# A six-stage transformer: the light sum, the dense attention's schedule and the first expert gathers reordered

## The reference, cut to what matters

```python
x = x + half * routed_ffn(norm(x))      # f1: light local attention (windows of 128, 8 heads of 64) + heavy attention on routed tokens
x = x + latent_attention(norm(x))       # la: causal, 16 heads of 8, rotary
x = x + half * routed_ffn(norm(x))      # f2: as f1
x = x + half * experts(norm(x))         # m1: 64 experts of up to 48 tokens, plus a shared ffn
x = x + cosine_attention(norm(x))       # ca: 16 heads of 8, q and k normalised, dense softmax over 512 keys, output bias bo
x = x + half * experts(norm(x))         # m2: as m1
```

## Time and profile before

| | |
|---|---|
| median of 3 runs | 3302.72 us (3302.44 to 3307.93) |
| the profiled execution's own time, its span | 3303.23 us, 3301.5 us |
| PE, DVE, ACT, POOL busy | 85%, 70%, 56%, 45% of the span |
| exponentials of f1l, of f2l (first to last start) | 65.4 to 525.0, 1601.6 to 2089.7 us |
| exponentials of la | 901.8 to 1534.4 us |
| scatters of m1, of m2 | 2487.3 to 2584.2, 3196.6 to 3293.2 us |
| exponentials of ca | 2675.7 to 3052.2 us |

### The profile page before, as it was taken

One profiled execution on the slowest core, in us unless ns is written; L12 is line 12 of the kernel. 1 busy time (PEld: TensorE's weight loads), 2 busy tenths in 40 slices (PEclk: granted clock), 3 DMA queues, 4 the chain that ended last, 5 costly groups with the idle time before them and its releaser, 6 DMA issues. The chain is left out here.

```text
span 3301.5 us, 72698 instructions
## 1 busy us (share of the span) xinstructions
PE 2797.7 (85%) x24552; PEld 1869.8 (57%) x24552; DVE 2312.4 (70%) x6126; ACT 1849.4 (56%) x3771; POOL 1476.8 (45%) x1662
## 2 busy tenths in 40 slices
PE   7999998997699999998888999799785278887774
PEld 4777886775233333333567777677663145555642
DVE  5887776884588888883677777599662267786641
ACT  3777664553166666664577666455541257776421
POOL 1222236883455555542122223578555354451445
PEclk9999998998599999998999999899895579999775
DMA  2000000001333333320000000000162255553532
GB/s 80 1 0 1 0 0 1 0 0 31 77 78 79 79 79 81 87 68 14 14 0 0 1 0 0 1 0 0 50 164 35 82 138 124 135 127 88 142 86 31
DMA packets 158029, 162.92 MB, mean 49 GB/s; under 512 B 43264, under 2 KB 136064, under 8 KB 157056
## 3 DMA queue, kind: packets, MB, share of 16 engines
q1 hardware_dynamic: 148032, 148.24, 17.5%
q0 software_dynamic: 9216, 7.87, 1.8%
q10 hardware_dynamic: 576, 4.19, 0.3%
HBM read 84.57 MB, written 74.60 MB: 48 GB/s over the span
## 5 line engine op out<-in xcount | busy, mean ns | idle before, releaser
L1721 DVE CUSTOM_DVE_ANT_0 la_ps<-la_ps,la_tri 128x512 f32<-128x512 f32 (+3 forms) x1024 | 480.4, 514 | 91.9 <-PE la_ps L1302 84.2
L1575 ACT ACTIVATE la_prob<-la_ps 128x512 f32<-128x512 f32 x640 | 374.0, 601 | 236.0 <-PE la_ps L1313 229.1
L371 POOL TENSOR_TENSOR f2l_prob<-f2l_prob,f2l_rec 128x512 f32<-128x512 f32 x128 | 132.2, 1054 | 364.2 <-DVE f2l_rec L550 364.2
L1202 POOL TENSOR_SCALAR_AFFINE_SELECT la_prob<-la_prob 128x512 f32<-128x512 f32 x256 | 159.4, 635 | 298.9 <-ACT la_prob L1575 298.7
L1302 PE MATMUL la_ps<-la_ks,la_qs 48*128 48x512 bf16 (+3 forms) x1024 | 255.3, 318 | 42.2 <-DVE la_mx L1721 26.9
L371 POOL TENSOR_TENSOR f1l_prob<-f1l_prob,f1l_rec 128x512 f32<-128x512 f32 x128 | 133.9, 1067 | 334.2 <-DVE f1l_rec L550 334.2
L1313 PE MATMUL la_ps<-la_qs,la_ks 50*128 50x512 bf16 (+3 forms) x1024 | 243.0, 311 | 4.4 <-ACT la_prob L1575 1.8
L1313 PEld LDWEIGHTS la_ps<-la_qs,la_ks 50*128 50x128 bf16 x1024 | 67.2, 94 | 234.3 <-ACT la_prob L1575 170.8
L1345 PE MATMUL la_ps_o<-la_prob,la_v 128*32 128x512 f32 (+3 forms) x2048 | 196.0, 456 | 0.0
L1719 DVE TENSOR_REDUCE ca_mx<-ca_ps 128x4 f32<-128x512 f32 x256 | 163.7, 680 | 39.8 <-PE ca_ps L1302 39.5
L1575 ACT ACTIVATE ca_prob<-ca_ps 128x512 f32<-128x512 f32 x256 | 140.4, 598 | 38.1 <-PE ca_ps L1313 36.2
(11 more groups left out here) (551 smaller groups left out, 7979.2 us busy)
## 6 DMA issues: line engine op xcount, KB each, us to landing
stack_image<-la_parts SPq DMA_DIRECT2D x192, 128.0 KB, 2.4
stack_image<-ca_parts SPq DMA_DIRECT2D x192, 128.0 KB, 2.3
la_qs<-stack_image SPq DMA_DIRECT2D x64, 192.0 KB, 3.5
la_ks<-stack_image SPq DMA_DIRECT2D x64, 192.0 KB, 4.4
ca_qs<-stack_image SPq DMA_DIRECT2D x64, 192.0 KB, 3.8
ca_ks<-stack_image SPq DMA_DIRECT2D x64, 192.0 KB, 4.8
gather_table<-m_xn SPq DMA_DIRECT2D x32, 256.0 KB, 2.3
gather_table<-m_pr SPq DMA_DIRECT2D x32, 128.0 KB, 2.3
```

What stands on the lines that cost most here:

```text
L371: nc.gpsimd.tensor_tensor(pr[:, g], pr[:, g], rc[:, g].rearrange("p (h o) -> p h o", o=1).broadcast_to([P, PAIRS, P]), ALU.mult).then_inc( ...
L1202: return nc.gpsimd.affine_select(view, view, pattern=[[0, 4], [1, P]], compare_op=ALU.is_ge, fill=0.0, base=0, channel_multiplier=-1)
L1575: nc.scalar.activation(prob[q % 2][:, n], ps2[n % 2][:], ACT.Exp, scale=SM).then_inc(S["p_sb"], 1)
L1721: last = nc.vector.tensor_tensor_reduce(bank[:, col:col + width], bank[:, col:col + width], tri[:, T - width:T], 1.0, -BIG, ALU.add, ALU.m ...
```

## The change

1. `light_attention`, DVE: the output sum y (L554) moves from behind the reciprocals to in front of the wait for the exponentials.
2. `stacked_attention`, dense form: the slots after every second unit become `place` after every unit, on PE, ACT and DVE, with the work spread over the 16 units; probabilities times v goes in two halves. The split of the maxima goes from DVE to POOL. The bias is added to y by POOL ahead of time (`add_bias`), and DVE's sum becomes one instruction; `added` goes. POOL's order in a body becomes one list. SP stores k's parts, loads the first half, sends the maxima rows, stores the next batch's q parts, then loads the second half. For the latent form only two empty instructions on POOL and some implied waits differ.
3. `moe_block`: SP writes the lists ahead of the store of base sum 12 and reads them back ahead of that of 13; POOL issues two gathers after each of base sums 13, 14 and 15.

The hunks of the dense attention are shown with the lines that stay and those that come; the lines that go are the `slot` functions and waits of the kernel as printed above.

```diff
@@ -541,6 +541,12 @@
                     if past(d, 1):
                         settle(d - 1)
                     descend(d)
+                if live(i, 3):
+                    dve.wait_ge(f_ps, i - 2)
+                    j = i - 3
+                    nc.vector.scalar_tensor_tensor(
+                        y[:, bass.ds(j, 1), :].rearrange("p o c -> p (o c)"), ps_a[:, 2], 0.5,
+                        x[:, bass.ds(j, 1), :].rearrange("p o c -> p (o c)"), ALU.mult, ALU.add).then_inc(y_ready, 1)
                 if live(i, 1):
                     dve.wait_ge(p_sb, i)
                     nc.vector.tensor_reduce(rsum[:], prob[(u - 1) % 2][:], X_AX, ALU.add).then_inc(sum_ready, 1)
@@ -548,12 +554,6 @@
                     if past(i, 3):
                         dve.wait_ge(norm_ready, 2 * i - 4)
                     nc.vector.reciprocal(rec[(u - 1) % 2][:], rsum[:]).then_inc(rec_ready, 1)
-                if live(i, 3):
-                    dve.wait_ge(f_ps, i - 2)
-                    j = i - 3
-                    nc.vector.scalar_tensor_tensor(
-                        y[:, bass.ds(j, 1), :].rearrange("p o c -> p (o c)"), ps_a[:, 2], 0.5,
-                        x[:, bass.ds(j, 1), :].rearrange("p o c -> p (o c)"), ALU.mult, ALU.add).then_inc(y_ready, 1)
                 if live(i, -2) and not late(i, r):
                     dve.wait_ge(xrT_ps, i + 2)
...
@@ -1141,26 +1140,39 @@
+                    if latent:
+                        store_parts(i + 2, u, 0)
+                    store_parts(i + 2, u, 1)
+                if latent and live(i, -1):
                     m_rows(i + 1, 1 - u, 0)
                 if live(i, -2):
                     sp.wait_ge(S["store_done"], 192 * (i + 3))
+                    load_half(i, u, 0)
+                if not latent and live(i, -1):
+                    m_rows(i + 1, 1 - u, 0)
+                if not latent and live(i, -3):
+                    store_parts(i + 3, 1 - u, 0)
+                if live(i, -2):
+                    load_half(i, u, 1)
+
+            def store_parts(b, u, t):
+                sp.wait_ge(S["part_ready"], 2 * b + 1 + t)
+                if t == 0 and past(b, 2):
                     for g in range(GROUPS):
+                        sp.wait_ge(load[g], 64 * (b - 1))
+                for blk, blks, part, stays in (RUNS_Q, RUNS_K)[t]:
+                    for k in range(blks):
+                        sp.dma_start(image[u, t, AD * (blk + k):AD * (blk + k + 1)].rearrange("d h t -> h d t"),
+                                     parts[:, t, part if stays else part + k]).then_inc(S["store_done"], 16)
+
+            def load_half(i, u, g):
+                if past(i, 0):
+                    sp.wait_ge(S["s2_ps"], UB * i + UB // 2 * (g + 1))
+                for t, stack in enumerate((qs[u], ks[u])):
+                    for s in range(2):
+                        r0, h0 = HALF_ROWS * s, PA * s + GP * g
+                        sp.dma_start(stack[r0:r0 + SROWS, GP * g:GP * g + GP, :], image[u, t, :, h0:h0 + GP, :])\
+                            .then_inc(load[g], 16)
 
             def m_rows(b, u, g):
                 sp.wait_ge(S["mT_sb"], 2 * b + 1 + g)
...
@@ -1228,16 +1242,27 @@
 
+            def add_bias(b):
+                pool.wait_ge(S["xn_ready"], b + 1)
+                nc.gpsimd.nop(nofuse=True)
+                ys = y[:, bass.ds(TPB * b, TPB), :]
+                nc.gpsimd.tensor_tensor(ys, ys, bo[:].broadcast_to([P, TPB, C]), ALU.add).then_inc(S["shifted"], 1)
+
             def body(i, u):
+                if not latent:
+                    if live(i):
+                        split_maxima(i, 1)
+                    if live(i, -2):
+                        split(i + 2, 1, 2, 5)
+                    if live(i, -1):
+                        split_maxima(i + 1, 0)
+                    if live(i):
+                        add_bias(i)
+                    if live(i, -3):
+                        split(i + 3, 0, 0, 5)
+                        split(i + 3, 1, 0, 2)
+                    return
                 for q in range(QUADS):
                     if live(i) and q == 0:
                         split_maxima(i, 1)
...
@@ -1473,62 +1508,49 @@
                 nc.tensor.matmul(ps_c[:], ones8[:], sq[:], start=True, stop=True).then_inc(S["sum_ps"], 1)
 
+            def place(i, u, q, n):
+                k = 4 * q + n
+                if k == 1:
                     if live(i):
                         m_t(i, 1)
                     if live(i, -3):
                         project(i + 3, 1 - u, 0)
+                if k == 4 and live(i, -3):
+                    project(i + 3, 1 - u, 1)
+                if k == 5 and live(i, -3):
+                    squares(i + 3, 0)
+                if k == 8:
                     if live(i, -3):
+                        squares(i + 3, 1)
                     if live(i, -1):
                         m_t(i + 1, 0)
+                if k == 9 and live(i, 1):
+                    turn_y(i - 1)
+                if k == 12 and live(i, 1):
+                    pe.wait_ge(S["yT_sb"], i)
                     if live(i, -3):
+                        pe.wait_ge(S["floored"], 2 * i + 8)
+                    else:
+                        pe.wait_ge(S["v_sb"], min(i + 2, B))
+                    for part in range(2):
+                        project_out(part)
+                if k == 13 and live(i, -4):
+                    xn_t(i + 4)
+                if n == 2:
+                    b, qb = (i, q - 2) if q >= 2 else (i - 1, q + 2)
+                    if live(i, 0 if q >= 2 else 1):
+                        otr(b, qb)
+                if n >= 2:
+                    b, qb, ub = (i, q - 1, u) if q else (i - 1, 3, 1 - u)
+                    if live(i, 0 if q else 1):
+                        pv(b, ub, qb, (0, 1) if n == 2 else (2, 3))
+                if k == 15 and live(i, -2):
+                    if live(i, -3):
+                        pe.wait_ge(S["floored"], 2 * i + 8)
                     if live(i, 1):
+                        pe.wait_ge(S["out_done"], i)
+                    for part in range(2):
+                        project_v(i + 2, u, part)
 
             def xn_t(b):
                 pe.wait_ge(S["xn_ready"], b + 1)
...
@@ -1608,21 +1629,28 @@
                 nc.scalar.copy(oT[:], ps_o[:]).then_inc(S["o_sb"], 1)
 
+            def place(i, u, q, n):
+                k = 4 * q + n
+                if k == 0 and live(i, -3):
+                    xnT_copy(i + 3, 1 - u)
+                if n == 0:
+                    b, qb = (i, q - 2) if q >= 2 else (i - 1, q + 2)
+                    if live(i, 0 if q >= 2 else 1):
+                        o_copy(b, qb)
+                if k == 2 and live(i, -3):
+                    biased(i + 3, 0)
+                if k in (3, 5) and live(i, -4):
+                    make_xn(i + 4, (k // 2 - 1,))
+                if k == 6 and live(i, -3):
+                    biased(i + 3, 1)
+                if k == 7 and live(i, -3):
+                    inverse(i + 3, 0)
+                if k == 9 and live(i, 1):
                     turned_y(i)
+                if k == 10 and live(i, -4):
+                    make_xn(i + 4, (2, 3))
+                if k == 11 and live(i, -3):
+                    inverse(i + 3, 1)
 
             def biased(b, t):
                 n = 2 * b + t
...
@@ -1707,7 +1735,7 @@
             def maxima(b, q, n):
-                if latent and n == 0 and q % 2 == 0 and past(b, 1):
+                if n == 0 and q % 2 == 0 and past(b, 1):
                     dve.wait_ge(S["m_ready"], 2 * b - 1 + q // 2)
                 dve.wait_ge(S["s1_ps"], UB * b + UQ * q + n + 1)
                 if latent:
...
@@ -1757,17 +1776,14 @@
                 out = ps_c[:].rearrange("p (a b) -> p a b", a=TPB)
+                if not latent:
+                    dve.wait_ge(S["shifted"], i)
+                    nc.vector.nop(nofuse=True)
+                nc.vector.tensor_tensor(ys, out, ys, ALU.add).then_inc(S["out_done"], 1)
 
...
@@ -1789,42 +1805,33 @@
 
+            def place(i, u, q, n):
+                k = 4 * q + n
+                if k == 1 and live(i):
+                    m_copy(i, 1)
+                if n == 3:
+                    b, qb = (i, q - 2) if q >= 2 else (i - 1, q + 2)
+                    if live(i, 0 if q >= 2 else 1):
+                        normalise(b, qb)
                 if k == 4 and live(i, -1):
+                    dve.wait_ge(S["v_ps"], i + 2)
+                    if live(i, 1):
+                        dve.wait_ge(S["pv_ps"], 4 * i)
+                    nc.vector.tensor_tensor(v[1 - u][:, :, :, 0:AD], ps_c[:].rearrange("p (j h d) -> p j h d", j=TPB, h=AH),
+                                            bv[:].rearrange("p o (h d) -> p o h d", h=AH).broadcast_to([P, TPB, AH, AD]),
+                                            ALU.add).then_inc(S["v_sb"], 1)
+                if k == 6 and live(i, -3):
+                    floor(i + 3, 0)
```

(32 more changed lines are left out.)

197 lines of the change are left out of this document (38 added, 159 removed).

## The result

The changed kernel took 3216.11 us in the median of 4 runs (3212.86 to 3218.55), the kernel before 3303.18 in the median of 4 beside them: the ratio is 0.9733, with a 95% interval from 0.9716 to 0.975. The profiled execution took 3215.8 us, 87.4 less than that of before. The forecast was 3224. The first row is the page's (busy us of each engine); the others are the exponentials of the two light blocks, first to last start.

What follows compares the result with a forecast made beforehand. It took DVE's ring, with PE in f2l's later passes, the first scatter's start, and PE's dense idle time as limits; 26 + 6 + 14 + 33 = 79 us off 3303.2, less 0.5, gave 3224 us, range 3188 to 3262.

Steps and rivals of the forecast that it cites:

- rivals A to D: A: dense body stays 24.5 us, 0.16; B: light gains only 9 us, 0.14; C: most idle returns, 0.08; D: slower, 0.07.
- 17 less 2.5: f2l descent: earlier make_xr and tmin gain 17 us; row sums standing behind y lose 2.5 us.
- Later passes: 0.30 x 39 = 12 us: f2l after the descent: PE's 0.30 us wait for y goes in 39 passes, gaining 12 us.
- Only if `make_xr` starts before POOL does ... I take the middle, 6: f1l descent: only an earlier make_xr start gains, 12 us; 6 taken, between a 2.5 loss and 12.
- this price of the gathers: Experts: sum 15, its store and gathers 5 and 6 come 2.6 us later, covered before the first scatter.
- The landing: Experts: the third gather, no longer beside the read-back, takes 3.5 us to land, so PE starts 7 us earlier.
- Half of PE's idle time: Dense attention: half of PE's lost 4.3 us a body recovered, 2.1 in each of 12 bodies, 25 us.
- start and tail: Dense attention: most of ACT's 7.87 us near the end with nothing from PE goes, 8 us.
- PE's waits for transfers: Dense attention: earlier loads remove PE's waits for the stacks from HBM, 15.3 us in 11 waits.
- DVE's 3.5 us: Dense attention: DVE loses maxima splits, one output sum and a port wait, about 3.5 of 19.4 us a body.
- Rival D: Dense attention: POOL's second maxima split runs late, delaying PE and SP's loads; body over 28.3 us, kernel slower; chance 0.07.
- Paced by DVE's 1024 maxima, and POOL is idle most of it: Latent attention: the waits removed, empty instructions and implied waits cost nothing there.

Runs made afterwards that it cites:

- one_product: The changed kernel with POOL's two light-attention products joined into one; 3239.17 us, ratio 0.9812 to the kernel before.
- sp_order_alone: The kernel before with only SP's new dense-attention order of stores and loads; 3292.97 us, ratio 0.9951 to the kernel before.
- splits_on_dve: The changed kernel with the dense splits of the maxima given back from POOL to DVE; 3215.52 us, ratio 0.9733 to the kernel before.
- loads_late: The changed kernel with the first half's dense loads issued behind the maxima's rows and the next q parts' store; 3365.07 us, ratio 1.0194 to the kernel before.
- sp_order_old: The changed kernel with all of SP's dense-attention order as before the change; 3226.29 us, ratio 0.9753 to the kernel before.
- xr_two_buffers: The changed kernel with a second xr buffer and make_xr moved ahead of the row sums; 3201.46 us, ratio 0.9694 to the kernel before.
- xr_before_y: The two-buffer xr kernel (make_xr ahead of the row sums) with make_xr moved again, ahead of y; 3193.57 us, ratio 0.9663 to the kernel before.

## Why the prediction was right, and where it was not

*Sum.* 79 us were forecast and 87.4 measured. By stage: f2l 32.2 (forecast 26), f1l 6.8 (6), experts 7.9 + 7.1 (14), dense 34.5, which is 32.0 in the exponentials' span and 2.5 ahead of it (33). All three parts hold alone. These are 88.5; the rest, 1.1, is the difference between unchanged stages. None of the rivals A to D came.

*f2l's descent passes: right.* The 27 intervals of the descent took 222.0 us before (the 28th exponential starts at 1823.61) and 206.0 after (1799.43): 16.0, forecast 17 less 2.5. The ends of `make_xr` and `tmin` are where they were put, and one_product shows the mechanism.

*Later passes: the mis-sized term.* "Later passes: 0.30 x 39 = 12 us" took PE's idle time from the earlier trace rows and left f1l's later passes at nothing. The rest of f2l fell from 266.1 to 249.8 us, 16.3, and that of f1l from 257.2 to 249.1, 8.1. The reader can see why in PE's timeline, of the kernel before, the same three lines as shown above of after:

```profile
1878.49 1.02 PE L420 MATMUL f2l_ps_v<-f_wqkv,f2l_xrT 128*128 128x512 f32 x2
1879.81 0.33 PE L425 MATMUL f2l_ps_a<-g_ident,f2l_xr 128*128 128x128 f32 x1 [0.30 <-DVE g_x L554]
1880.07 1.16 PE L433 MATMUL f2l_ps_s<-f2l_qkT 64*128 64x128 f32 x16
```

The profile calls the idle time 0.30, but from L420's start to L425's it is 1.32 us, and 0.86 after: 0.46 from there, and 0.06 more to L433. Busy time of pipelined matmuls overlaps where they follow one another, so an idle time in the listing is less than what the wait costs. The pace, 7.37 us a pass in the median, fell to 6.84, and f1l's 7.07 to 6.83, so that neither was PE's own pace.

*f1l: right by its number, wrong by its mechanism.* The step "Only if `make_xr` starts before POOL does ... I take the middle, 6" did not bring a gain: in five descent passes `make_xr` did start before POOL by the listing, 0.01 to 0.03 us, and was held as in the others. The descent part went from 202.4 to 203.7 us, a loss of 1.3 (2.5 were allowed), and all of the gain is that of the later passes, which the forecast had at nothing. That 6.8 came out so near 6 is luck. Whether a won race would have shortened a pass with two products no run shows; in one_product it was won in 19 passes of 24, and there `tmin` was held in its place.

*Experts: right.* 7 a block; base sum 15 came 2.4 us later (56.7 us behind base sum 0 instead of 54.35), and this price of the gathers was hidden as said. The landing took 4.0 us where 3.5 were taken. That both moves are needed was not said.

*Dense: right by the body (22.4 forecast, 22.07), the reason only in part.* Half of PE's idle time came back, 2.43 x 12 = 29 us (25 forecast), and 5 at start and tail (8 forecast). The half was a choice, and that it fits is in part luck. The text put it on PE's waits for transfers and on DVE's 3.5 us; sp_order_alone shows that the waits did not set the body, and splits_on_dve that 1.3 of the 3.5 us do not matter in the new order. The placement of the pieces on PE, ACT, DVE and POOL, the bias among them, brought all of the 2.4 us; SP's order added nothing to an even body and kept one long one away. Which of the moved pieces did it was not taken apart further, so this cause stays open. Rival D's place is real, as loads_late shows (SP's queue behind POOL's late parts cost 10 us a body, the fall of the granted clock included), but the order that was written keeps clear of it.

*The latent attention: no cost, but not for the reason given.* Its exponentials span 632.5 us before and 630.0 after. "Paced by DVE's 1024 maxima, and POOL is idle most of it" does not fit the trace of before: from 901 to 1534 us PE is busy for 609 us, DVE for 529 and POOL for 328, which is half of it.

## What to carry to other kernels

Price a stall from start to start of the instructions on either side of it, in a pass with the stall and one without, not by the idle time in the listing, and look at every pass that has it. Where two engines share a port, list the ends of each short instruction against the other's long ones: moving the short one in front of the long one helps only until the next one is caught, so follow the ring to its next limit. Where two chains meet before the first result, move both or neither. Look at single bodies before a mean is put down to an edit: the 0.5 us by which sp_order_old's mean body is longer was one body of nine. In a queue that serves several stages ask first what each issue makes the next one wait for.

## What the runs showed of the hardware that was not expected

- POOL is held by DVE too: in xr_two_buffers, where `tmin` gets in between the two products, the pair takes 2.22 us; with `make_xr` between them it takes 2.08, and with nothing 2.04.
- With the two listed starts less than 0.1 us apart `make_xr` takes 0.35 or 2.09 us, and the passes of f1l in one_product scatter from 7.58 to 8.49 us within one run. A listed lead of 0.01 to 0.05 us does not tell who is held.
- In xr_before_y DVE's reduction that reads PSUM (L534, 1.21 us) and the small sums of 48 rows (L528, 0.25 to 0.27 us) kept their durations beside POOL's products.
- A short wait of PE can cost more than itself: behind one of 2.09 us (sp_order_old, at 2728.71) the granted clock was 0.50 from 2729 to 2735 us, and the body took 4.4 us more than its neighbours (PE busy 23.5 us in it instead of 20.6).
